# A four-image tower of attention and expert blocks: one common set of PSUM banks, first loads in order of need, a later turn, and unwaited adds within an expert

## The reference, cut to what matters

```python
h = tok(x)                                   # relu(x W0) * (x W1), times Wo, 512 hidden
h = ln(h + attn0(h))                         # 16 heads of 16, window of +-64 keys
h = ln(h + ffn0(h))                          # quantised: rows to 8 bits, weights to -1/0/1
h = ln(h + attn1(h))                         # 16 heads of 16, causal
h = ln(h + experts(h))                       # top 2 of 8 experts, 640 rows each, silu, ln inside too
```

## Time and profile before

| | |
|---|---|
| median of 3 runs | 1139.83 us (1137.66 to 1139.97) |
| the profiled execution: its own time | 1142.34 us |
| the profiled execution: its span | 1140.6 us |
| PE busy, mean granted clock | 891.3 us (78%), 0.888 |
| DVE, ACT, POOL busy | 554.3 (49%), 422.8 (37%), 297.1 us (26%) |
| first matmul | 12.04 us |
| first scores | 57.39 us |
| last matmul ends, last instruction | about 1088.5 us, 1140.6 us |

### The profile page before, as it was taken

How to read it: one execution, slowest core, us unless ns; L and a number is a source line. 1 busy time by engine, 2 the same in 40 slices (tenths; PEclk the granted TensorE clock), 3 DMA queues, 4 the chain that set the end, 5 groups by cost and what they waited for, 6 DMA issues and landing times. The chain is left out here.

```text
span 1140.6 us, 14091 instructions
## 1 busy us (share of the span) xinstructions
PE 891.3 (78%) x4838; PEld 552.0 (48%) x4838; DVE 554.3 (49%) x2103; ACT 422.8 (37%) x717; POOL 297.1 (26%) x364
## 2 busy tenths in 40 slices
PE   5685989967867867977988778742999999999910
PEld 2443445524524534524534424231677777777810
DVE  3256424668668767768786777341021112111227
ACT  1213423556556565666635535400312211122002
POOL 4000311413413412302324242405011122112322
PEclk9987989979989988979989979665999999999965
DMA  5585550540440550540555330106213442243242
GB/s 179 82 178 192 56 76 1 58 56 1 57 56 2 57 56 1 58 56 1 57 80 87 45 73 21 38 19 235 76 18 112 120 125 67 68 116 65 24 97 74
DMA packets 58664, 80.96 MB, mean 71 GB/s; under 512 B 6753, under 2 KB 50658, under 8 KB 56161
## 3 DMA queue, kind: packets, MB, share of 16 engines
q1 hardware_dynamic: 48944, 67.19, 30.3%
q0 software_dynamic: 7296, 9.47, 5.1%
q10 hardware_dynamic: 2352, 3.40, 0.9%
HBM read 35.36 MB, written 19.15 MB: 48 GB/s over the span
## 5 line engine op out<-in xcount | busy, mean ns | idle before, releaser
L1004 DVE CUSTOM_DVE_ANT_0 junk<-ps,maskb 128x256 bf16<-128x256 f32 (+4 forms) x512 | 207.1, 435 | 120.3 <-PE ps L725 117.8
L553 ACT ACTIVATE probs<-ps 128x512 f32<-128x512 f32 (+1 forms) x304 | 159.5, 548 | 106.8 <-PE ps L748 101.5
L1465 PE MATMUL ps<-dxT,w1s 128*128 128x320 f32 x512 | 141.1, 436 | 2.4 <-DVE dxT L1529 2.3
L1477 PE MATMUL ps<-w2s,hTe 128*128 128x256 f32 x640 | 139.3, 379 | 0.0
L725 PE MATMUL ps<-ks,qs 96*128 96x256 bf16 (+4 forms) x512 | 113.6, 301 | 26.8 <-DVE nmax L1004 12.3
L1477 PEld LDWEIGHTS ps<-w2s,hTe 128*128 128x128 f32 x640 | 121.1, 190 | 16.3
L1499 ACT ACTIVATE hTe<-ps,b1s 128x640 f32<-128x640 f32 x64 | 50.8, 795 | 204.5 <-PE ps L1465 204.5
L1424 POOL DMA_INDIRECT mixed_rows<-ysb,ids x40 | 61.8, 1544 | 238.4 <-DVE ysb L1547 140.6
L748 PE MATMUL ps<-qs,ks 99*128 99x256 bf16 (+4 forms) x512 | 112.5, 306 | 10.8 <-DMA qs<-nrows 7.0
L1465 PEld LDWEIGHTS ps<-dxT,w1s 128*128 128x128 f32 x512 | 98.0, 192 | 43.5 <-DVE dxT L1529 2.9
L460 POOL TENSOR_SCALAR_AFFINE_SELECT probs<-probs 128x256 f32<-128x256 f32 (+1 forms) x64 | 39.3, 615 | 245.9 <-ACT probs L553 245.8
(11 more groups left out here) (164 smaller groups left out, 1195.5 us busy)
## 6 DMA issues: line engine op xcount, KB each, us to landing
qs<-parts SPq DMA_DIRECT2D x96, 128.0 KB, 4.8
ks<-parts SPq DMA_DIRECT2D x96, 128.0 KB, 7.5
w1s<-w SPq DMA_DIRECT2D x8, 1024.0 KB, 9.4
w2s<-w SPq DMA_DIRECT2D x8, 1024.0 KB, 4.9
dispatched_rows<-oT SPq DMA_DIRECT2D x20, 260.0 KB, 6.6
dx<-dispatched_rows SPq DMA_DIRECT2D x8, 650.0 KB, 7.5
x_sb<-xT SPq DMA_DIRECT2D x8, 256.0 KB, 6.3
h<-wq SPq DMA_DIRECT2D x2, 1024.0 KB, 10.2
```

What stands on the lines that cost most here:

```text
L553: act.activation(probs_of(u)[:, heads[0]:heads[-1] + 1, :], turned_bank((u, half, i))[:, 0:len(heads) * w].rearrange("p (j n) -> p j n", n=w),
L1004: ins = dve.tensor_tensor_reduce(out=junk[:, S_UNIT[u, half, i] % NS, a * (hi - lo):(a + 1) * (hi - lo)], in0=score_bank((u, half, i))[:, ...
L1465: ins = mm(bank(2 * (n % 2) + c)[:, 0:HC], w1s[:, e % 2, k, m * P:(m + 1) * P], dxT[:, e % 2, k, c * HC:(c + 1) * HC], start=(k == 0), sto ...
L1477: ins = mm(bank(4 + n % 2)[:, 0:D], hTe[:, e % 2, m, t * P:(t + 1) * P], w2s[:, e % 2, m, :], start=(m == 0), stop=(m == MH - 1))
```

## The change

It does these things:

1. The scores, `back` and all dense units take from one set of five banks (0, 1, 2, 6, 7); at each unit the one used longest ago is taken, so they go round in the order in which PE opens them. The transposed scores keep banks 3 and 4.
2. All first loads but the constants go to SP's queue in order of need. The three weights of the feed-forward get three staging buffers (a slot of `qs`, a part of `probs`, and the old one), and are loaded at the start. PE's wait for the constants moves to the first `wq` phase, DVE's for the attention weights to half -8. A `wq` phase has four steps: the sum over partitions and ACT's scaling move to its third step, the rounding to its fourth.
3. The zeros are written in 8 DMAs, four from half -19 on and four from half 3 on, and the padding rows of the result become 640, in one DMA. The buffer of zeros moves from `oT` to `att`; the wait for them moves from ACT to DVE, at the first `heads`.
4. The turn of the quantised rows, with ACT's copy, moves from step 2 of a feed-forward phase to the early part of step 3, behind that half's scores.
5. POOL waits before an add only at the first tile of an expert, for all adds of the expert before. Each padding place of an expert has now its own padding row.

```diff
-STEPS = {"tok": 12, "qkv": 8, "o": 6, "ffn": 16, "gate": 2, "route": 12, "bias": 2, "wq": 3}
+STEPS = {"tok": 12, "qkv": 8, "o": 6, "ffn": 16, "gate": 2, "route": 12, "bias": 2, "wq": 4}
-FQT, FIRST_TILE, PER_TILE = 2, 3, 2
+FQT, FIRST_TILE, PER_TILE = 3, 3, 2
...
+V_BANK, BANKS = 5, 8
+def banks_for(kind, n):
+    return {"s": (0, 1, 2, 6, 7), "t": (3, 4), "d": (0, 1, 2, 6, 7)}[kind]
+
+def take(kind, n, key):
+    b = min(banks_for(kind, n), key=lambda i: LAST_USE[i])
+    AT[kind, key] = (b, USES[b])
+    USES[b] += 1
+    LAST_USE[b] = len(AT)
...
@@ staging buffers and zeros
+            wst = [v[:, 2, :, :].rearrange("p h n -> p (h n)").bitcast(F32) for v in (qs,)]
+            wst.append(probs[:, 4 * P * HG:4 * P * HG + KD * I0])
+            wst.append(h3[:, 2 * NT:4 * NT, :].rearrange("p t d -> p (t d)")[:, 0:KD * I0])
+            zero_rows = att[...][:, 0:CT * DX]
...
@@ sync
                     sp.dma_start(tokwo[:, :, :], wtok).then_inc(for_tok, 16)
+                    sp.dma_start(aw[0][:, :, :], wattn[0]).then_inc(for_a0, 16)
+                    sp.dma_start(ab[0][:, :], battn[0]).then_inc(for_a0, 16)
+                    sp.dma_start(mask_in, masks).then_inc(for_mask, 16)
+                    for l in range(2):
+                        sp.dma_start(awo[l][:, :, :], wo[l]).then_inc(for_rest, 16)
+                        sp.dma_start(bvc[l][:, :], bvcol[l]).then_inc(for_rest, 16)
+                        sp.dma_start(ar[l][:, :], brow[l]).then_inc(for_rest, 16)
+                    for i in range(3):
+                        sp.dma_start(wst[i], wdn if i == 2 else wq0[i]).then_inc(w_in[i], 16)
+                    sp.dma_start(aw[1][:, :, :], wattn[1]).then_inc(for_rest, 16)
+                    sp.dma_start(ab[1][:, :], battn[1]).then_inc(for_rest, 16)
+                    sp.dma_start(gatew[:, :, :], wgate).then_inc(for_rest, 16)
...
+                        if part == 0 and q == NR - 1 and not is_k:
+                            sp.wait_ge(w_taken, 1)
...
-                        if 3 <= eta < 13:
-                            zeros(2 * (eta - 3), 2 * (eta - 3) + 2)
+                        if eta == -19:
+                            sp.wait_ge(prep_pool, 4)
+                        if -19 <= eta < -15:
+                            zeros(eta + 19)
+                        if 3 <= eta < 7:
+                            zeros(eta + 1)
...
@@ scalar
+                        if u == 2 and half == 0:
+                            act.wait_ge(w_taken, 2)
-                        if g == 0:
-                            act.wait_ge(zeroed, 16 * (ROWS // (2 * P) + 1))
...
                     def early(phase, i, c):
+                        if phase == "ffn" and c == FQT:
+                            both(("ffn", i, "fqT"), fqT, BF16)
...
@@ tensor
+                    def opened(kind, key):
+                        b, n = AT[kind, key]
+                        if n:
+                            pe.wait_ge(read[b], n)
+                        return bank(b)
...
                     def early(phase, i, c):
+                        if phase == "ffn" and c == FQT:
+                            pe.wait_ge(fq_done, i + 1)
+                            o = d_open(("ffn", i, "fqT")).bitcast(BF16)
+                            for n in range(2 * NT):
+                                ins = pe.transpose(o[:, n * P:(n + 1) * P], fqb[:, n * P:(n + 1) * P],
+                                                   identb[:, :])
+                            ins.then_inc(d_full(("ffn", i, "fqT"))[0], 1)
...
-                    pe.wait_ge(for_cst, 16)
-                    pe.wait_ge(prep, 2)
                     for eta in HALVES:
...
@@ vector
-                    dve.wait_ge(for_a0, 16 * 2)
-                    ab_q = ab[0][:, :].rearrange("p (b c) -> p b c", c=2)[:, :, 0:1]
-                    dve.tensor_scalar(ab_q, ab_q, DH ** -0.5, None, ALU.mult).then_inc(prep, 1)
...
+                        if g == 0:
+                            dve.wait_ge(zeroed, 16 * (E + 1))
...
                     for eta in HALVES:
+                        if eta == -8:
+                            dve.wait_ge(for_a0, 16 * 2)
+                            ab_q = ab[0][:, :].rearrange("p (b c) -> p b c", c=2)[:, :, 0:1]
+                            dve.tensor_scalar(ab_q, ab_q, DH ** -0.5, None, ALU.mult).then_inc(prep, 1)
...
@@ second block, gpsimd
                             pool.wait_ge(y_done, e * CT + t + 1)
-                            if e or t:
-                                pool.wait_ge(y_out, 16 * (e * CT + t))
+                            if e and t == 0:
+                                pool.wait_ge(y_out, 16 * CT * e)
```

More of the change, by code:

```diff
@@ L129, in dense_units @@
     if phase in ("bias", "wq"):
-        return ("one",) if c == 1 else ()
-    if c == FQT:
-        return ("fqT",)
+        return ("one",) if c == (1 if phase == "bias" else 2) else ()
     down, half, turn = tile_at(c, DOWN), tile_at(c, 0), tile_at(c, TURN)
@@ L138, in early_units @@
 def early_units(phase, c):
-    t = tile_at(c, 1) if phase == "ffn" else None
+    if phase != "ffn":
+        return ()
+    if c == FQT:
+        return ("fqT",)
+    t = tile_at(c, 1)
     return () if t is None else (f"gb{t}", f"ub{t}")
@@ L153 @@
         for _i, _ in enumerate(score_heads(_n // 2, _n % 2)):
-            S_UNIT[_n // 2, _n % 2, _i] = len(S_UNIT)
+            take("s", _n, (_n // 2, _n % 2, _i))
+    for _phase, _i, _c in SCHED.get(_n, ()):
+        for _key in early_units(_phase, _c):
+            take("d", _n, (_phase, _i, _key))
     if (_n - TO_ROWS) % 8 == 0 and 0 <= _n - TO_ROWS < 2 * UNITS:
-        T_UNIT["n", (_n - TO_ROWS) // 8] = len(T_UNIT)
+        take("t", _n, ("n", (_n - TO_ROWS) // 8))
     if 0 <= _n - TO_TURNED < 2 * UNITS:
@@ L231, in bank @@
             return ps[:, i, :]
-        x_in, for_tok, for_a0, for_rest, for_cst, for_mask, mask_done, w_in, w_taken = (
-            sem(n) for n in ("x_in", "for_tok", "for_a0", "for_rest", "for_cst", "for_mask", "mask_done", "w_in", "w_taken"))
+        x_in, for_tok, for_a0, for_rest, for_cst, for_mask, mask_done, w_taken = (
+            sem(n) for n in ("x_in", "for_tok", "for_a0", "for_rest", "for_cst", "for_mask", "mask_done", "w_taken"))
         for_gu = [sem(f"for_gu{i}") for i in range(2)]
+        w_in = [sem(f"w_in{i}") for i in range(3)]
         prep = sem("prep")
@@ L243, in build @@
         wa_in = sem("wa_in")
[L246 to L248 removed]
+        filled, read = ([sem(f"{n}{i}") for i in range(BANKS)] for n in ("filled", "read"))
         pv_mm, ot_done, sel_done, nparts_done, max_chain = (
@@ L653, in dense @@
                             act.activation(pp[:, 0, :, :], rt[:, :, :], ACT.Exp).then_inc(raised, 1)
-                        if phase == "wq" and c == 1:
+                        if phase == "wq" and c == 2:
+                            if i == 0:
+                                act.wait_ge(prep_pool, 1)
                             act.wait_ge(w_scaled, i + 1)
-                            act.activation(wst, wst, ACT.Identity, bias=magic[:, 0:1],
+                            act.activation(wst[i], wst[i], ACT.Identity, bias=magic[:, 0:1],
                                            scale=wsc[:, 8 + i:9 + i]).then_inc(w_raised, 1)
@@ L942, in dense @@
                             ins.then_inc(d_full(("bias", i, "one"))[0], 1)
-                        if phase == "wq" and c == 1:
+                        if phase == "wq" and c == 2:
+                            if i == 0:
+                                pe.wait_ge(for_cst, 16)
+                                pe.wait_ge(prep, 2)
                             pe.wait_ge(w_sum, i + 1)
@@ L1004, in maximum @@
                                 ins = dve.tensor_tensor_reduce(
-                                    out=junk[:, S_UNIT[u, half, i] % NS, a * (hi - lo):(a + 1) * (hi - lo)],
+                                    out=junk[:, AT["s", (u, half, i)][0], a * (hi - lo):(a + 1) * (hi - lo)],
                                     in0=score_bank((u, half, i))[:, a * (hi - lo):(a + 1) * (hi - lo)], in1=mask,
```

119 lines of the change are left out of this document (43 added, 76 removed).

## The result

| | before | after |
|---|---|---|
| median of the runs, us | 1139.9 | 1111.69 (1110.21 to 1113.61) |
| the profiled execution: time / span, us | 1142.34 / 1140.6 | 1110.42 / 1108.6 |
| mean granted clock | 0.888 | 0.895 |

The ratio is 0.974, 95% interval 0.9688 to 0.9793: 28 us less by the medians, 32.0 by the spans of the two profiles, where 43.4 was forecast.

The account below looks back on a forecast made before the run. PE bounds the experts; from 57 to 710 us no engine is full and waits decide, DVE bounding the weights stage after the change. Terms 4.8 + 12.4 + 10 + 4 + 2 + 10.2 = 43.4 off 1139.8 give 1096.4 us, range 1078 to 1114.

Parts of the forecast that it names:

- rival A: Banks worth nothing, ACT and DVE being the chain; start, weights and adds stay: -27.4, 1112.4 us; chance 0.24.
- Start, -4.8: Before PE's first matmul: needed loads go first, so PE starts at 7.2 us, not 12.04; bounds 3.5 and 5.5.
- The named covers: At the start: DVE's product runs freely during POOL's memset; SP's added DMAs finish by 31 us, 5 us before parts' transfers.
- Weights, -12.4: 57 to 112 us: DVE's 9.3 us load waits go and sums are hidden; halves 4 to 15 take 29 us, not 41.4.
- Banks, -10, -4 and -2: 112 to 710 us: common banks save 10 us in feed-forward phases, 4 at scores, 2 of half-clock time.
- The chain I worked out: Feed-forward tile: with PE ahead, ACT and DVE need 7.1 us between L676 starts, 0.7 us less a tile.
- The -4 of the scores: Of PE's 18.3 us waits to open scores, 112 to 710 us, 4 us go; bounds 0 and 18.
- The clock's -2: 112 to 710 us: half-clock stretches after bank waits shrink, giving 2 us; bounds +10 and -12.
- Coupling (C): Common ring: score units wait for late dense readers; at 0.1 us over 352 units, slower, 1147.6 us; chance 0.04.
- My sign of being wrong: The forecast is wrong if L791's bank waits, 33.5 us before, stay under a new name, a score's reader.
- Turn, 0: Feed-forward phases: moving the quantised rows' turn later changes nothing, DVE's chain staying; bounds +2 and -2 for all four.
- Adds, -10.2: Tail on POOL: last add starts 0.32 us after its data and lands at 1093.5, not 1103.7; bounds 0 and 10.5.

Follow-up runs that it names:

- experiment 1: Changed kernel with the banks of before (scores 0 to 2, dense 6 and 7): 1119.91 us, ratio 0.9778 to the kernel before.
- experiment 4: Changed kernel with first loads of attention weights, masks and biases back on ACT's queue, early feed-forward weight loads kept: 1113.73 us, ratio 0.9731 to the kernel before.
- experiment 5: Changed kernel with the three feed-forward weights loaded late as before, four steps kept: 1123.97 us, ratio 0.9822 to the kernel before.
- experiment 9: Changed kernel with early weight loads kept but a weight's phase back to three steps: 1109.54 us, ratio 0.9713 to the kernel before.
- the second profile: Profile of the changed kernel run a second time, unaltered, in experiment 11: span 1110.3 us against 1108.6 in the first.
- experiment 8: Changed kernel with the second and third wq phases one and two halves earlier: 1108.32 us, ratio 0.9686 to the kernel before.
- experiment 10: Changed kernel with the edits of experiment 7 and experiment 8 together: 1103.99 us, ratio 0.9664 to the kernel before.
- experiment 6: Changed kernel without ACT's square of the gate in all four feed-forward phases (relu(g)*u computed): 1095.81 us, ratio 0.9579 to the kernel before.
- experiment 7: Changed kernel with a `back` unit's bank counted as used three turns later: 1106.34 us, ratio 0.9667 to the kernel before.
- experiment 2: Changed kernel with the turn of the quantised rows and ACT's copy back in step 2: 1109.58 us, ratio 0.9698 to the kernel before.
- experiment 3: Changed kernel with POOL waiting before each add for the one before: 1120.47 us, ratio 0.9793 to the kernel before.
- experiment 11: Changed kernel once more, unaltered, as control: 1111.03 us, ratio 0.9726 to the kernel before.

## Why the prediction was right or wrong

The time fell inside the range, 15 us above the forecast's own, and next to the 1112.4 us of rival A. But that rival's mechanism is false: experiment 1 gives the common banks 7 to 10 us. A's total is right by accident: what the banks brought is about what the weights stage, the start and the experts fell short.

**Start, -4.8: right.** -4.4 measured in these two profiles, -2.9 to -4.9 over all profiles with the changed start; the first matmul is at 7.33 us where 7.2 was forecast, and experiment 4 moves it back to 11.98. The 0.7 us from the last needed byte to the semaphore, of which no row was shown, was near: SP's queue had moved the needed 1.0 MB by 6.3 us, and the second DMA of `tokw` landed at 7.19. By 8 us the transfers have moved as much as before (216 GB/s over those 8 us against 222 in the earlier trace rows), so it is the order alone. The named covers held: DVE's product was not held up by POOL's memset (0.69 us in the middle of it), and SP issued the last zeros 20 us before the parts.

**Weights, -12.4: too much; -8.2 measured.** The first part of the step held: the waits of DVE on loads are gone, and taking the loads late again costs 12.5 us (experiment 5). The term held 29 us for halves 4 to 16, which took 34.7 (41.4 before); the first four halves gave 1.5 us that I had not counted. The part that failed is "two halves between sum and PE's use hide the 2.29 us of the sum". I counted halves and didn't look how long they last. Half 13's scores start at 84.9 us, half 14's at 85.6, because nothing dense stands in them. DVE meanwhile is behind with the weight before and starts the third sum at 88.09:

```profile
82.48 0.16 DVE L1332 TENSOR_SCALAR wsc<-ps 128x1 f32<-128x1 f32 x1 [3.08 <-PE ps L978]
85.00 1.23 DVE L1339 TENSOR_SCALAR probs<-probs 128x2048 f32<-128x2048 f32 x1 [1.29 <-ACT probs L688]
...
88.09 2.28 DVE L1327 TENSOR_REDUCE wsc<-h 128x1 f32<-128x2048 f32 x1
...
90.42 0.59 PE L978 MATMUL ps<-wsc,cst 128*128 128x4 f32 x2 [4.35 <-DVE wsc L1327]
```

PE comes for it at 86.07 and stands 4.35 us. I had set DVE's 25.4 us of work beside PE's and summed each as if it could flow freely; it is their order that bunches them. DVE is behind because it stood itself: the second sum was done at 78.0 us, but its sum over partitions (L978) now comes a half later, in PE's list behind the `tok` output matmuls (L862), and was through only at 82.5. So DVE waited 3.08 us for PE and then 1.29 us for ACT's scaling, and started the third sum late. That the fourth step made this detour is read from the order of the lists; experiment 9 shows only that without the step the stage is shorter. A second miss is in the clock: I let PE's work in these halves fall to 22 us, at full clock. It did not: PE is busy 25.86 us from half 4 to half 16, against 26.60 in the earlier trace rows, at a mean clock of 0.83, and stands at half clock for 11.9 us of them (9.3 in the second profile) against 13.7 before. Moving the weight phases closer together brought that down to 6.8 and 2.5 us (experiments 8 and 10). The fourth step, which my text credited with hiding the sum, costs the stage 2.4 us or more (experiment 9); with late loads the kernel is 4.3 us over before's three steps in this stage (experiment 5).

**Banks, -10, -4 and -2: the mechanism right, the sizes not; -10.6 in all, -8.2 by the second profile.** The feed-forward phases gave 4.6 us, from 208.3 to 203.7 (6.4 by the second profile), where 10 was forecast. The chain I worked out, ACT and DVE at 7.1 us a tile, is real (experiment 6), but a tile takes 8.07 us in the mean, not 7.1, and before it took 8.44, not the 7.67 and 7.99 that I read off one phase. The failed step is the 7.1, and in it the words "with PE ahead". PE is not always ahead: over the twelve stretches from one L706 to the next, ACT stands 6.9 us before its relu (L611) waiting for PE's L821, 0.6 us a tile (7.4 us before, 4.4 in the second profile, 3.2 in experiment 7), the 2.63 us shown under experiment 7 among them. ACT also serves others in between: in the tile from 323.28 to 331.07 us, 7.79 long, with PE ahead, it copies the rows of split maxima (L562, 0.57 us), which my sum leaves out, and idles 0.24 us between its two gates, where I had 0.15 us for all gaps. Single tiles take from 7.04 to 9.72 us, and I took one phase's tiles for all. The -4 of the scores is not shown: outside the feed-forward phases halves 16 to 255 are 6.0 us shorter in one profile and 1.8 in the other, but experiment 1, with split banks, has the same 390 us there as experiment 2 with common ones. The clock's -2 is not shown: PE is at half clock for 109.8 us of that stretch before and for 107.5 and 110.1 in the changed kernel's two profiles. Experiments 3 and 4, whose code in that stretch is the same, have 120.4 and 98.1 us. What the Trainium skill tells of its example (TensorE: Matmul & The Clock Gate, "HAM oscillation — how this bites in real kernels"), no further gain from more PSUM buffering, does not hold for this kernel: the common banks gave 7 to 10 us.

**Coupling (C): not the outcome, but present.** I asked it to hit 352 score units at 0.1 us each. That way it hit four times in halves 16 to 255, for 2.5 us together (L755 behind L1210). It hit more the other way about: dense units waited for attention units' readers eight times, 12.2 us together. My sign of being wrong, "if L791's waits stay under a new name (a score's reader)", is there in part. One of the eight, of 3.3 us, is shown to cost: the first feed-forward phase, which alone had gained nothing, gains 3.6 us without it (experiment 7). My argument, "the unit five back is a half old, and its reader has mostly passed", is true of most units, and these waits are its exceptions.

**Turn, 0: right** (experiment 2). The wait at the turn grew by 5.9 us over all, and the span didn't.

**Adds, -10.2: right.** -10.3 behind the last matmul, 10.0 back with experiment 3. The last add started 0.28 us after its data and landed 3.78 us later, against 0.32 and 3.84 in my sum.

**Not foreseen:** +1.0 us from half 255 to the experts and +0.6 in them. From kernel to kernel the first varies between 75.3 and 78.3 us, with no edit that bears on it, and I leave it there.

Added up: 0.4 short at the start, 4.2 in the weights, 5.4 in the banks and the clock, 1.6 behind them, 0.1 over in the tail: 11.5 us, the 43.4 less the 32.0 of the profiles, to rounding. By the medians it is 28.2: before's profiled execution was 2.4 us over its median, the changed kernel's 1.3 under.

## What to carry to other kernels

When a bank or buffer wait goes, don't count it as gained before looking at what the engine waits for next in its list, data above all: here 30.1 us of waits for the shared banks left PE, 22.4 us came back further down its list, some 15 of them for data, and 7 to 10 us was the gain. Before pricing "a step more hides X", look up how long that step lasts at the place where it is used: a step of the list that holds nothing but its scores lasted 0.6 us, where the mean of halves 0 to 16 is 2.9. And a step more also delays what hangs on it, and here the stage was shorter without it. And when two kinds of work share one ring, look for the units that wait for the other kind's reader, and keep the slowest reader's bank out longest: one line brought 3.6 us.

## What the runs showed of the hardware that was not expected

- An accumulating indirect DMA of 128x256 elements holds POOL 1.54 us and lands 3.78 us after its start (3.6 to 7.8 over the 40). Two can be in flight at once, though all go to one tensor through one queue: started 3.45 us apart, and once 2.42, they still land after 3.78 us. Where each waits for the one before (the kernel before, experiment 3), the last ones start 4.4 to 4.6 us apart.
- Loads on a second queue hold up those on the first, though the first issues its own at the same times: with the later-needed loads on ACT's queue the second DMA of `tokw`, on SP's, issued at 2.4 us in both kernels, lands at 11.85 us instead of 7.19, while the bytes moved by 8 us are the same within 3%.
- The same matmuls of halves 8 to 16 took 18.04 us at a mean clock of 0.78 and 15.74 us at 0.85. Two profiles of the changed kernel alone differ there by 0.78 to 0.82. The change took 6.4 us of waits for sums out of this stage, and the time at half clock in halves 4 to 16 fell from 13.7 us to 11.9 and 9.3; experiment 8 took 1.3 us more of waits out, and it fell to 6.8. Why so much less the first time was not tried.
- The time at half clock is no steady property of a piece of code: halves 16 to 255, the same in experiments 3, 4 and 11, stood at half clock for 120.4, 98.1 and 110.1 us, while the stretch took 593.1, 591.2 and 593.0 us.
